# Second layer's key splits moved into units 0 to 3, first negation and first values moved in the cross attention

## The reference

```python
x = x + cross_attention_0(layernorm(x), ctx, mask)   # 16 heads of 8, 128 queries, 2048 keys
x = x + latent_attention_0(layernorm(x))             # causal, 16 heads
x = x + (layernorm(x) @ W[idx] + b[idx])             # idx: argmax of a Gumbel choice
x = x + cross_attention_1(layernorm(x), ctx, ctx)
x = x + self_attention_1(layernorm(x))
x = x + moe(layernorm(x))                            # 16 experts, 4 chosen, and a shared one
```

## Time and profile before

| what | value |
|---|---|
| time, median of 3 runs | 333.61 us (333.51 to 333.7) |
| the profiled execution's own time | 331.68 us |
| its span in the profile | 329.7 us |
| TensorE (PE) busy | 285.2 us, 87% |
| VectorE (DVE) busy | 231.8 us, 70% |
| ScalarE (ACT) busy | 206.7 us, 63% |
| GpSimd (POOL) busy | 71.5 us, 22% |
| mean granted clock of TensorE | 0.928 |

### The profile page before, as it was taken

The page is one execution under the profiler, slowest core; times in us unless marked ns, Lnnn a source line. Parts: engine busy times, 40 slices in busy tenths (PEclk is TensorE's granted clock), DMA queues, the critical chain, the costliest instruction groups (busy, mean ns, idle before and its releaser), DMA issues.

```text
span 329.7 us, 10086 instructions
## 1 busy us (share of the span) xinstructions
PE 285.2 (87%) x4246; PEld 186.9 (57%) x4246; DVE 231.8 (70%) x374; ACT 206.7 (63%) x423; POOL 71.5 (22%) x136
## 2 busy tenths in 40 slices
PE   7847999999999997889648899999999984894886
PEld 5334566667676644735315566767666653342655
DVE  5935899999999835363556899999999803714572
ACT  4572698988989872324402698988989870251141
POOL 5792500000000025220360630000000000300033
PEclk9996999999999998799965999999999995899599
DMA  7943325522224505220000025422231000000000
GB/s 256 414 158 116 126 74 203 174 76 79 72 88 126 213 2 191 95 89 12 0 0 0 2 75 175 165 75 84 66 90 60 3 2 0 2 2 0 0 2 16
DMA packets 10688, 27.84 MB, mean 84 GB/s; under 512 B 2209, under 2 KB 3169, under 8 KB 10258
## 3 DMA queue, kind: packets, MB, share of 16 engines
q1 hardware_dynamic: 10568, 26.97, 24.4%
q10 hardware_dynamic: 74, 0.20, 0.2%
HBM read 20.74 MB, written 6.42 MB: 82 GB/s over the span
## 4 chain that ended last, share of the span: by engine, by line
PE 69%; DVE 14%; issue 8%; ACT 3%; DMA 3%; POOL 2%; SPq 1%; DVEq 0%; POOLq 0%
PE bank L932 67%; DVE mx L698 4%; DVE s_neg L767 1%; DMA k_scratch<-kparts 1%; DMA kpair<-k_scratch 1%; DVE kparts L668 1%; POOL y L324 1%; DVE xn L656 1%; DVE k_rest L665 1%; PE bank L1152 1%; PE bank L963 1%; ACT probs L470 0%; ACT xnT L423 0%; DVE v_all L758 0%; SPq L236 0%
## 5 line engine op out<-in xcount | busy, mean ns | idle before, releaser
L698 DVE TENSOR_REDUCE mx<-bank 128x2 f32<-128x1024 f32 x128 | 154.4, 1224 | 21.7 <-PE bank L932 18.0
L470 ACT ACTIVATE probs<-bank 128x512 f32<-128x512 f32 x256 | 139.4, 595 | 18.2 <-PE bank L932 14.0
L932 PE MATMUL bank<-q_exp,kpair 64*128 64x128 bf16 x1024 | 84.9, 217 | 1.3 <-ACT probs L470 0.5
L932 PE MATMUL bank<-kpair,q_rows 64*128 64x512 bf16 x256 | 74.6, 394 | 8.6 <-DMA kpair<-k_scratch 7.1
L932 PE MATMUL bank<-probs,v_all 128*9 128x128 f32 x2048 | 79.9, 274 | 1.1 <-ACT probs L470 1.0
L932 PEld LDWEIGHTS bank<-q_exp,kpair 64*128 64x128 bf16 x1024 | 55.7, 94 | 31.6 <-issue 15.0
L932 PEld LDWEIGHTS bank<-probs,v_all 128*9 128x9 f32 x2048 | 43.2, 90 | 15.3 <-ACT probs L470 4.0
L361 POOL CAST m_rows<-negm 128x2 bf16<-128x2 f32 x32 | 6.2, 193 | 154.4 <-DVE negm L705 154.4
L932 PEld LDWEIGHTS bank<-kpair,q_rows 64*128 64x128 bf16 x256 | 22.7, 94 | 10.4 <-issue 7.8
L423 ACT ACTIVATE v_all<-bank 128x512 f32<-128x512 f32 (+1 forms) x18 | 10.1, 575 | 23.8 <-PE bank L932 23.8
L324 POOL TENSOR_TENSOR y<-ve,mhalf 128x2 f32<-128x2 f32 x6 | 4.2, 695 | 54.1 <-DVE ve L647 54.1
(11 more groups left out here) (209 smaller groups left out, 348.9 us busy)
## 6 DMA issues: line engine op xcount, KB each, us to landing
k_scratch<-kparts SPq DMA_DIRECT2D x24, 256.0 KB, 2.9
kpair<-k_scratch SPq DMA_DIRECT2D x63, 96.0 KB
kpair<-k_scratch SPq DMA_DIRECT2D x63, 64.0 KB
ctxT_s<-in_ctxT SPq DMA_DIRECT2D x4, 512.0 KB, 6.6
mask_s<-in_mask SPq DMA_DIRECT2D x2, 1024.0 KB, 10.7
kpair<-k_scratch SPq DMA_DIRECT2D x63, 32.0 KB
wM<-in_packM SPq DMA_DIRECT2D x1, 1728.0 KB, 7.1
wB<-in_packB SPq DMA_DIRECT2D x1, 727.0 KB, 6.4
```

Source lines behind the costliest of these rows:

```text
L470: act.activation(probs[:, j % 4, :], bank[:, 4 + j % 2, :], ACT.Exp).then_inc(S("exp_done"), 1)
L698: V.tensor_reduce(mx[n % 2][:, w, :], bank[:, 2 * (w % 2):2 * (w % 2) + 2, :], AX.X, ALU.max) \
L932: return T.matmul(out_, lhsT=lhsT, rhs=rhs, start=start, stop=stop, **kw)
```

## The change

Three places change. In layer 2 all four `split_k` move into the unit loop, one behind the `m_rows` of each of units 0 to 3 (`K_LATE` from (1, 2) to (1, 4)). `negate(0)` moves in front of the maximum of window (1,0), in both layers. In layer 1, chunk 3 of the values moves ahead of the first score window, chunks 4 to 7 move up to stand behind score windows 2 to 5, and nothing stands behind `put_exp(0)` any more; the banks of chunks 3 to 7 change with it, and the first two `b_unit`s now both wait for all eight chunks.

```diff
--- before.py
+++ after.py
@@ -35,9 +35,9 @@
 Q_BANK = (0, 1, 4, 5)
 WARM = 36
 EARLY_BANK = ((2, 3, 6, 7), (2, 3, 2, 3))
-V_BANK = ((2, 3, 6, 4, 5, 7, 4, 5), (7, 6, 7, 6, 4, 5, 7, 4))
+V_BANK = ((2, 3, 6, 7, 4, 5, 7, 4), (7, 6, 7, 6, 4, 5, 7, 4))
 V_EARLY = (3, 4)
-K_LATE = (1, 2)
+K_LATE = (1, 4)
 U = 4
 E = 16
 FB = E * 64 // P
@@ -478,11 +478,9 @@
                     act.activation(gum[:, 33:34], gum[:, 32:33], ACT.Ln).then_inc(S("gum_lse"), 1)
                     act.wait_ge(S("gum_lse"), 1)
                     act.activation(gum[:, 62:63], gum[:, 33:34], ACT.Exp, scale=-1.0)
-                for c in range(V_EARLY[l], 8 - (l == 0)):
+                for c in range(V_EARLY[l], 8):
                     prep_v(l, c)
                 put_qe(0)
-                if l == 0:
-                    prep_v(0, 7)
                 for n in range(NN):
                     for j in range(8):
                         exp_unit(n, j)
@@ -721,10 +719,9 @@
                         put_rows(l, k)
                 for w in range(4):
                     maxima(0, w)
+                negate(0)
                 for w in range(2):
                     maxima(1, w)
-                    if w == 0:
-                        negate(0)
                 for n in range(NN):
                     if n + 1 < NN:
                         maxima(n + 1, 2)
@@ -1015,7 +1012,7 @@
                     if j == 0:
                         pe.wait_ge(S("qe_put"), g0 + n + 1)
                     if n == 0 and j < 2:
-                        pe.wait_ge(S("v_copied"), 8 * (l + 1) - (l == 0 and j == 0))
+                        pe.wait_ge(S("v_copied"), 8 * (l + 1))
                     if 8 * (g0 + n) + j >= 2:
                         pe.wait_ge(S("exp_done"), 8 * (g0 + n) + j - 1)
                     for t in range(4):
@@ -1049,15 +1046,15 @@
                 k1_at = {(14, 3): 0, (15, 0): 1, (15, 1): 2, (15, 2): 3}
                 pe.wait_ge(S("q_rows"), 2 * (l + 1))
                 pe.wait_ge(S("q_rows2"), 2 * (l + 1))
+                if l == 0:
+                    prep_v(0, V_EARLY[0])
                 for i, (n, w) in enumerate([(0, 0), (0, 1), (0, 2), (0, 3), (1, 0), (1, 1)]):
                     a_ready(n, w)
                     a_head(n, w, 0)
                     a_head(n, w, 1).then_inc(S("a_done"), 1)
                     if 1 <= i < 5:
-                        prep_v(l, V_EARLY[l] + i - 1)
+                        prep_v(l, 3 + i)
                 put_exp(0)
-                if l == 0:
-                    prep_v(0, 7)
                 for n in range(NN):
                     for k in range(4):
                         an, aw = (n + 1, 2 + k) if k < 2 else (n + 2, k - 2)
```

## The result

The changed kernel took 328.23 us (median of 4 runs, 327.35 to 329.32) where the kernel before took 333.56 in the same comparison: 5.3 us faster, ratio 0.987 (0.983 to 0.991). 327.9 was forecast. A second comparison gave 327.01 against 334.11, ratio 0.981 (0.977 to 0.986). Executions more than 1.5% above the fastest of their kernel (1262.26 us in x1_splits, 334.27 in x2_negate, which is the profiled one, 590.13 in x9_both, 475.88 of the kernel before beside the last four) are left out of the ratios, though not out of the medians. The profiled execution took 327.35 us (span 325.3) against 331.68 (329.7): 4.33 us less. The helper's line L932 is L929 now, L698 is L696, and VectorE's normalization is L650 to L654.

What follows compares the result with a forecast made beforehand. TensorE was taken to bound the kernel, with units of 5.33 us unchanged. Savings ahead of unit 0, 4.68 us in layer 2 and 1.03 in layer 1, together 5.7, took the median from 333.61 to 327.9; range 325.3 to 330.3.

Steps and rivals of the forecast that it cites:

- Edit 1, the normalization: Fourth normalization, ahead of layer 2's unit 0: without GpSimd's splits beside it, VectorE's instructions take 0.92 instead of 3.47, saving 2.55 us.
- Edit 1, the cast and the projection: Layer 2's query path: the cast without a split beside it saves 0.59 us, the projection at 2.4 GHz saves 0.52.
- The placing: Placing of layer 2's query: taken to stay at 1.2 GHz, nothing saved, with 0.63 us as upper end.
- Edit 1, nothing paid in units 0 to 3: Layer 2's units 0 to 3: the moved splits, 3.8 us each within units of 5.33, cost zero.
- D: Rival: the splits did not slow the fourth normalization, only the negations and chunk count gain; 332.1 us, 4%.
- E: Rival: the splits' cost moves to the units, holding VectorE in units 2 and 3; slower, 335.2 us, 4%.
- Edit 2: Start of both cross attentions: early negation ends the wait for m_rows; 0.52 us saved in layer 2.
- Edit 3: Layer 1's start: chunk 3 hides in the 7.10 us wait for keys; 1.03 us saved together with Edit 2.
- The cold stretch: Layer 2, first scores to first b_unit: an earlier clock rise saves 0.5 us, between 0 and 1.1.
- The sum: Whole kernel: 4.68 us in layer 2 plus 1.03 in layer 1, 5.7 saved; 326.4 to 329.3 given 60%.
- B: Rival: the clock does better, with fast placing, shortest start stretch and a shorter later one; 7.9 saved, 325.7 us, 15%.
- C: Rival: the clock gives nothing or takes back, a later cold stretch growing by up to 1 us; 329.5 us, 14%.

Runs made afterwards that it cites:

- x1_splits: The kernel before with only the key splits changed: all four of layer 2 in units 0 to 3; 328.03 us, ratio 0.984.
- x2_negate: The kernel before with only the negation moved ahead of the fifth maximum; 331.97 us, ratio 0.995.
- x9_both: The changed kernel with the wait for the first value copies behind chunk 3, and unused matmuls ahead of layer 2's unit 0; 324.8 us, ratio 0.973.
- x5: The changed kernel with one split of layer 2 ahead of unit 0 instead of none; 329.98 us, ratio 0.991.
- x4: The changed kernel without its branch on the mask and the masked form of layer 1's cross attention; 327.42 us, ratio 0.981.
- x3: The kernel before with only chunk 3 of layer 1's values moved ahead of the first scores; 333.13 us, ratio 1.000.
- x7: The changed kernel with the wait for the first three value copies moved from ahead of the branch to behind chunk 3; 327.0 us, ratio 0.984.
- a0: The changed kernel again, unaltered, in a second comparison; 327.01 us, ratio 0.981.
- x6: The changed kernel with chunk 3 of layer 1's values moved ahead of the branch; 327.95 us, ratio 0.987.
- x11: The changed kernel with chunk 3 of layer 1's values back behind the second score window, chunk 7 behind put_exp(0), old banks; 328.02 us, ratio 0.981.
- x10: x9_both with further unused matmuls in TensorE's gaps between the layers and behind layer 2; 320.5 us, ratio 0.959.
- x8: The changed kernel with 36 unused matmuls in TensorE's gaps ahead of layer 2's unit 0; 324.27 us, ratio 0.975.

## Why the prediction was right, step by step

**Edit 1, the normalization: right.** 3.74 to 1.19 us is 2.55, the forecast figure. x1 and x5 show that the splits did it.

**Edit 1, the cast and the projection: right.** 0.52 for the cast (0.59 forecast), 0.52 for the projection. The placing stayed at 1.47, as taken.

**Edit 1, nothing paid in units 0 to 3: right.** The windows and the store's slack show it. Rivals D and E are refuted, by x1 and by these windows. The premise that an earlier start moves all behind it by as much holds for the units, but not past them: x4's 0.98 us were gone at the fourth normalization.

**Edit 2: right.** From the first scores to layer 2's first `b_unit` it took 10.1 to 10.2 us with the late negation and a late rise of the clock (before, x3), 9.3 to 9.6 with the early one (after, x2, x4, x7); with an early rise 8.80 (x1) and 8.2 to 8.4 (a0, x5, x6, x11). Where the clock rose alike the difference is 0.6 either way: 10.21 (x3) against 9.62 (after), both with the rise at 6.3 us, and 8.80 (x1) against 8.19 (x11), both at 3.0 to 3.1. 0.52 was forecast.

**Edit 3: the step that failed.** "TensorE had waited 7.10 us for the keys' load ..., so it hides." The row named the load because that was what ended last. Under it lay the branch: the copies ended at 20.8 in the trace before, and 5.5 us of branch put TensorE at about 26.3, 0.7 us before the keys:

```profile
19.20 1.57 ACT L423 ACTIVATE v_all<-bank 128x512 f32<-128x512 f32 x3
```

The instruction packet says the same: it ended at 24.55 there, and 1.7 us behind it is 26.3. So the cover was about 0.7 us (0.36 by the changed kernel's 26.62 against 26.98 for the keys), and the chunk takes 2.0. It was no loss because the same matmuls only changed places: from TensorE's first matmul behind the branch to the first `b_unit` it is 9.46 us (26.62 to 36.08), against 9.50 before, with the clock's rise 3.4 and 3.5 us into it. The 0.5 us of edit 2 are given back in there: TensorE now waits 0.37 us for `q_exp`, which chunk 7 had covered. Where the clock rose 5.0 us into it, the same stretch is 10.18 with edits 2 and 3 (x5) and 9.58 with edit 2 and without 3 (x11). Of the 1.03 forecast for layer 1, 0.40 came: 0.36 from the earlier first matmul and 0.04 from the stretch. Where the cover is real the forecast holds: in x4 the first scores to the first `b_unit` take 8.33 us, and the prediction had 8.47 (26.98 to 35.45).

**The cold stretch: mis-sized.** "I take the middle, 0.5 saved": the profiled execution saved nothing (6.3 us from the first scores to the rise, 6.0 before), another of the same kernel saved more than all (a0: 2.9 us, stretch 8.18). Its range is 1.4 us, not 1.1. Over all traces edit 1 does shift it. In the three kernels with both splits ahead of unit 0 (before, x2, x3) the clock was low for 13.7 us there; in the eight traces with one split or none and no unused matmuls (after, a0, x1, x4 to x7, x11) it was low for 10.2 or 6.8. So a rule by which these stretches are not the change's to give is too strong here, with one profile for each kernel but the changed one.

**The sum.** Forecast 5.7; the trace has 0.40 + 4.25 - 0.25 = 4.4; the medians 5.3 and 7.1 (6.3 by the ratio). That the first median lies 0.3 us from the forecast is in part luck: the step that failed was 0.6 us too much, the cold stretch 0.5, and the two medians differ by more than either. Eleven of the twelve kernels and the kernel before have a cold stretch between the layers, of 6.8 to 13.7 us, and most of the work in it is TensorE's. The Trainium skill, TensorE: Matmul & The Clock Gate, Part 1: The HAM clock gate, says that the point of warming varies from run to run. The traces agree: the changed kernel warmed 6.3 us behind layer 2's first scores in one execution and 2.9 in another. The page gives ±500 ns for the variation, and the 3.3 us measured here are far more. The stretches that rivals B and C gave to layer 2's start were thus those of the same kernel in different executions; the fast placing of B was seen in no trace without unused matmuls. That these stretches are the whole spread of the medians wasn't shown; x10, which removes most of them, still spreads over 4 us. What fills the branch's 5.5 us ahead of the instruction packet and the 1.7 us behind it is open as well.

## What to carry to other kernels

A long idle time names only the wait that ended last. Before hiding work in it, ask when the engine's own stream would have been ready, and whether a branch or a wait lies under the named one; an experiment that takes the branch away tells. Look at what the other engine does beside a GpSimd instruction rather than at how much GpSimd does: two splits beside a normalization and a cast cost 3.7 us with what the clock added, and the same two beside reductions cost nothing. Where a start moves by 1 us, the clock of TensorE can take it back tens of us later; unused matmuls in the gaps and one moved wait (x10) were worth 6.5 us here, nearly as much as the change beside it (7.1).

## What the runs showed of the hardware that was not expected

- TensorE's branch between two code forms cost 5.5 us of issue (5.2 to 6.4 in the other four traces with the same waits), in which nothing ran on it. A 16 KB packet on the instruction queue ended 1.6 to 1.7 us before its first matmul in all eight traces where nothing else was waited for.
- A VectorE instruction of 0.16 us took 1.00 beside a GpSimd subtraction of 1.15.
- TensorE's clock stayed at 2.4 GHz through layer 2's start with 1.3 to 1.7 us of unused matmuls in each of three gaps (x8), and the stretch of 9.62 us became 6.92.
- An earlier start can go with an earlier fall of the clock: 0.98 us won at 36 was gone at 162, and the clock had fallen at 125.7 instead of 129.1 (x4).
